# A transformer layer in one kernel: where the reciprocal square roots of its two norms are made

## The reference

```
q = [x@Wq1, x@Wq2]   (2 x 16 heads of 16)     k, v = x@Wk, x@Wv
p = softmax(causal(q @ k^T / 4))              y = y1 - sigmoid(x@Wlam) * y2,  y1, y2 = halves of p @ v
x1 = norm(x + y @ Wo)
shared = (silu(x1@G) * (x1@U)) @ Down   (1024 wide)
routed = the same at 128 wide, times the sum of the softmaxed two largest router logits
out = norm(x1 + shared + routed)
norm(z) = (z - mean(z)) / sqrt(var(z) + 1e-5)   over the 256 features of a token
```

## Time and profile before

| | |
|---|---|
| time, median of 3 runs | 504.79 us |
| profiled execution, its time | 504.88 us |
| its span, first to last instruction | 503.1 us |
| TensorE busy | 424.3 us (84%) |
| VectorE busy | 329.1 us (65%) |
| ScalarE busy | 239.1 us (48%) |
| GpSimd busy | 226.7 us (45%) |
| one iteration, 2 to 6 | 54.2 us |
| mean granted TensorE clock | 0.95 |

### The profile page before, as it was taken

How to read it: one execution, slowest core, us unless ns; L and a number is a source line. 1 busy time by engine, 2 the same in 40 slices (tenths; PEclk the granted TensorE clock), 3 DMA queues, 4 the chain that set the end, 5 groups by cost and what they waited for, 6 DMA issues and landing times.

```text
span 503.1 us, 10443 instructions
## 1 busy us (share of the span) xinstructions
PE 424.3 (84%) x4008; PEld 337.4 (67%) x4008; DVE 329.1 (65%) x875; ACT 239.1 (48%) x532; POOL 226.7 (45%) x283
## 2 busy tenths in 40 slices
PE   4107597799999999999899999999999988997983
PEld 4106335676688758876798668865887578766983
DVE  3504615974478577877687677857786769676674
ACT  4601284337435672548334843576255821582240
POOL 8201466427435572547434743656254721373040
PEclk9756779889999999999999999999999999999998
DMA  8892496129603680249112940377024910000000
GB/s 290 188 123 49 126 137 150 44 75 124 89 4 114 91 121 23 75 92 135 51 42 78 141 90 12 107 97 119 20 79 74 133 46 0 5 2 22 1 23 21
DMA packets 34355, 40.43 MB, mean 80 GB/s; under 512 B 3840, under 2 KB 27904, under 8 KB 34048
## 3 DMA queue, kind: packets, MB, share of 16 engines
q1 hardware_dynamic: 34304, 39.75, 43.2%
HBM read 27.94 MB, written 11.53 MB: 78 GB/s over the span
## 4 chain that ended last, share of the span: by engine, by line
PE 69%; DVE 15%; DMA 5%; ACT 5%; issue 4%; POOL 2%; SPq 1%; DVEq 0%
PE ybank L734 10%; PE ff L622 9%; PE ff L624 8%; PE ff L623 8%; DVE neg_max L990 8%; PE ring L706 5%; PE ring L685 5%; DMA k_stack<-qk_parts_dram 4%; PE ybank L622 4%; PE ybank L747 3%; PE ring L710 3%; PE ybank L623 3%; PE ybank L624 3%; ACT prob L469 2%; PE ring L680 2%
## 5 line engine op out<-in xcount | busy, mean ns | idle before, releaser
L990 DVE TENSOR_REDUCE neg_max<-ring 128x2 f32<-128x512 f32 (+3 forms) x176 | 105.7, 635 | 39.2 <-PE ring L685 37.4
L469 ACT ACTIVATE prob<-ring 128x512 f32<-128x512 f32 x192 | 100.8, 612 | 15.9 <-PE ring L706 15.8
L370 POOL TENSOR_TENSOR h_lo<-h_full,h_hi 128x256 fp32r<-128x256 f32 x72 | 53.0, 736 | 107.7 <-ACT h_hi L429 107.7
L380 POOL TENSOR_SCALAR_AFFINE_SELECT prob<-prob 128x512 f32<-128x512 f32 x128 | 83.9, 679 | 33.9 <-ACT prob L469 33.9
L622 PE MATMUL ff<-x1T_hi,wg_lo 128*128 128x256 f32 x288 | 85.8, 298 | 1.2 <-DVE h_full L1006 1.2
L624 PE MATMUL ff<-x1T_hi,wg_hi 128*128 128x256 f32 x288 | 80.5, 279 | 0.0
L623 PE MATMUL ff<-x1T_lo,wg_hi 128*128 128x256 f32 x288 | 80.5, 279 | 0.0
L680 PE MATMUL ring<-mask_b,ident_b 128*128 128x128 bf16 (+2 forms) x176 | 45.2, 257 | 32.7 <-DMA k_stack<-qk_parts_dram 26.8
L477 ACT ACTIVATE gate_t<-ff 128x256 f32<-128x256 f32 x72 | 27.6, 384 | 77.2 <-PE ff L624 74.5
L685 PE MATMUL ring<-k_stack,q_stack 96*128 96x256 bf16 (+3 forms) x512 | 60.5, 239 | 0.0
L734 PE MATMUL ybank<-prob,v_ones 128*32 128x256 f32 (+1 forms) x1024 | 56.1, 338 | 4.2 <-issue 2.8
(11 more groups left out here) (150 smaller groups left out, 947.9 us busy)
## 6 DMA issues: line engine op xcount, KB each, us to landing
q_stack<-qk_parts_dram SPq DMA_DIRECT2D x48, 256.0 KB, 9.2
qk_parts_dram<-parts SPq DMA_DIRECT2D x72, 128.0 KB
k_stack<-qk_parts_dram SPq DMA_DIRECT2D x8, 384.0 KB, 15.0
xt_raw<-xT SPq DMA_DIRECT2D x8, 256.0 KB, 2.9
k_stack<-qk_parts_dram SPq DMA_DIRECT2D x8, 256.0 KB, 11.8
xz<-x SPq DMA_DIRECT2D x8, 256.0 KB, 3.3
out<-xz SPq DMA_DIRECT2D x8, 256.0 KB, 2.2
prob<-w_gu SPq DMA_DIRECT2D x1, 1152.0 KB, 7.7
```

Of the source, the lines that this page charges most:

```text
L370: pool.tensor_tensor(h_lo[:, n, :], h_full[:, n % RING, :], h_hi[:, n, :].bitcast(F32), ALU.subtract).then_inc(h_lo_done, 1)
L380: pool.affine_select(out=v, in_=v, compare_op=ALU.is_ge, fill=0.0, base=0, pattern=[[0, 2], [HALF, 2], [0, 2], [1, HALF]], channel_multipl ...
L469: act.activation(prob[:, g % RING, u, :], ring[u][:, :], ACT.Exp, scale=SCALE).then_inc(exp_done, 1)
L990: dve.tensor_reduce(neg_max[:, columns.start:columns.stop, i], ring[u % RING][:, 0:len(columns) * keys].rearrange("p (h k) -> p h k", k=keys),
```

## The change

GpSimd makes both reciprocal square roots. A constant tile `minus_half` (128x2, filled with -0.5) is added, and the root is one TENSOR_TENSOR with the operation `pow` of variance + EPS and that tile. The seed, the Newton steps and the shift of VectorE go; VectorE keeps statistics, aggregation and the application of the second norm.

```diff
+            def first_scale(b):
+                base = b * SCALE_STEPS
+                pool.wait_ge(attn_step, (b + 1) * ATTN_STEPS)
+                if not is_first(b):
+                    pool.wait_ge(x1_done, b * TT)
+                pool.tensor_scalar(ln_t[:, 0, 0, :], ln_mv[:, 0, :, 1], 1.0, EPS, ALU.mult, ALU.add).then_inc(norm1_scale, 1)
+                pool.tensor_scalar(ln_t[:, 0, 2, :], ln_mv[:, 0, :, 0], -1.0, 0.0, ALU.mult, ALU.add).then_inc(norm1_scale, 1)
+                pool.wait_ge(norm1_scale, base + 2)
+                pool.tensor_tensor(ln_t[:, 0, 1, :], ln_t[:, 0, 0, :], minus_half[:, :], ALU.pow).then_inc(norm1_scale, 1)
+                pool.wait_ge(norm1_scale, base + 3)
+                pool.tensor_tensor(ln_shift[:, :], ln_t[:, 0, 2, :], ln_t[:, 0, 1, :], ALU.mult).then_inc(norm1_scale, 1)
+
+            def second_scale(b):
+                pool.wait_ge(norm2_step, (b + 1) * LN_STEPS)
+                if not is_first(b):
+                    pool.wait_ge(out_done, b * TT)
+                pool.tensor_scalar(ln_t[:, 1, 0, :], ln_mv[:, 1, :, 1], 1.0, EPS, ALU.mult, ALU.add).then_inc(norm2_scale, 1)
+                pool.wait_ge(norm2_scale, 2 * b + 1)
+                pool.tensor_tensor(ln_t[:, 1, 1, :], ln_t[:, 1, 0, :], minus_half[:, :], ALU.pow).then_inc(norm2_scale, 1)
...
             def iteration(i, has_next, has_prev, has_last):
+                if has_prev:
+                    first_scale(i - 1)
                 if has_next:
                     split_xt(i + 1)
...
                     causal(i, range(g, g + 1))
+                    if has_last and g == SCALE_GROUP:
+                        second_scale(i - 2)
...
-            h_rests(B - 1, range(FF_UNITS))
+            first_scale(B - 1)
+            h_rests(B - 1, range(SCALE_UNIT))
+            second_scale(B - 2)
+            h_rests(B - 1, range(SCALE_UNIT, FF_UNITS))
+            second_scale(B - 1)
...
-                act.wait_ge(attn_step, (b + 1) * ATTN_STEPS)
+                act.wait_ge(norm1_scale, (b + 1) * SCALE_STEPS)
...
-                        if u < NEWTON + 4:
-                            first_norm_step(u, *before)
+                        if u == 0:
+                            norm_mean(0, *before)
...
-                        elif g <= NEWTON:
-                            norm_newton(1, *norm2)
-                        elif g == NEWTON + 1:
-                            second_norm_end(i - 2, *norm2)
+                        elif g == SCALE_GROUP + 2:
+                            second_norm_end(i - 2)
```

More of the change, by code:

```diff
@@ L52 @@
 ROUTER_STEPS = 5
-NEWTON = 3
-LN_STEPS = 2 * TT + 3 + (TT + 1) * NEWTON
-NORM1_STEPS = LN_STEPS + 1
+LN_STEPS = 2 * TT
+NORM1_STEPS = LN_STEPS
+SCALE_STEPS = 4
+SCALE_GROUP, SCALE_UNIT = 3, 2
 V_COLS = 32
@@ L87 @@
 EPS = 1e-5
-RSQRT_SEED = float(0x5F3759DF - 0x400000)
 F32 = mybir.dt.float32
@@ L92 @@
 BF16 = mybir.dt.bfloat16
-I32 = mybir.dt.int32
 ALU = mybir.AluOpType
@@ L146, in build_layer @@
         ln_shift = sb("ln_shift", [P, TT])
-        ln_i = sb("ln_i", [P, 2, TT], I32)
+        minus_half = sb("minus_half", [P, TT])
         gate_t = sb("gate_t", [P, RING, T])
@@ L207, in build_layer @@
         attn_step = sem("attn_step")
+        norm1_scale, norm2_scale = sem("norm1_scale"), sem("norm2_scale")
         gu_full, gate_th_done, gate_done, h_done, h_hi_done, h_lo_done = (sem(n) for n in ("gu_full", "gate_th_done", "gate_done", "h_done", "h_hi_done", "h_lo_done"))
@@ L333, in _ @@
             pool.memset(v_ones[:, :, :, HEAD_DIM:V_COLS], 0.0).then_inc(const_step, 1)
-            pool.wait_ge(const_step, STACKS + 4)
+            pool.memset(minus_half[:, :], -0.5).then_inc(const_step, 1)
+            pool.wait_ge(const_step, STACKS + 5)
             for m in (ident, ident_b):
@@ L940, in norm_mean @@
                     step(dve.bn_aggr(ln_mv[:, which, t, :], ln_stats[:, which, t, :]))
[L942 to L975, removed]
             def split_xt(b):
@@ L1090, in second_norm_start, with second_norm_end @@
                 norm_mean(1, step, settle)
[L1091 to L1095, removed]
+            def second_norm_end(b):
+                dve.wait_ge(norm2_scale, 2 * (b + 1))
                 z = xz[b % X_SLOTS]
@@ L1171, in _ @@
             first = stepper(attn_step, B * ATTN_STEPS - NORM1_STEPS + TT)
-            for n in range(NEWTON + 4):
-                first_norm_step(n, *first)
+            norm_mean(0, *first)
             x1T_second(B - 1)
@@ L1185, in _ @@
                     second_norm_start(B - 2, *norm2)
[L1186 to L1189, removed]
+                if n == SCALE_UNIT + 2:
+                    second_norm_end(B - 2)
             add_shared(B - 1, ring[0])
@@ L1193, in _ @@
             second_norm_start(B - 1, *norm2)
-            for _ in range(NEWTON):
-                norm_newton(1, *norm2)
-            second_norm_end(B - 1, *norm2)
+            second_norm_end(B - 1)
 _OUT = ((B, T, D), "float32")
```

## The result

The changed kernel takes 519.73 us (median of 4 runs, 519.17 to 520.39), against 504.75 us of the kernel before (4 runs too, one more than stood ahead of the prediction). The ratio is 1.030, 95% interval [1.028, 1.033]. So it is 3% slower: the forecast had the sign, but 3.7 us of loss where 15.0 were measured. The profiled run took 520.19 us with a span of 518.4 us, 15.3 us longer than before.

The account below looks back on a forecast made before the run. PE was taken to bound the kernel in iterations 2 to 6, VectorE in iteration 1. Losses of 10.2 + 0.5 us less gains of 7.0 made net +3.7 on 504.88 us: 508.5 us, range 503.5 to 521.

Parts of the forecast that it names:

- the rival on the slow power: GpSimd's pow is a software routine costing 1.3 us or more on two columns: 514.2 to 520.5 us; chance 0.17.
- The wait that is added: GpSimd's input split queues behind the first norm's root, so PE stalls 0.74 + C in each of iterations 2 to 6.
- C: Time of GpSimd's four new instructions, from the aggregation's end to the split's start: 1.3 us, with pow at 0.5.
- that half of the rival: A one-time load of about 6 us at pow's first call, stalling iteration 1: 514.5 us; chance 0.03.
- the formula 7C - 5.4: Net change of the whole kernel in us, losses less gains, as a function of C; break-even at 0.77 us.
- Iteration 1: VectorE bound it; without the norm steps and the half clock level it gains 4.2 - C, here 2.9 us.
- Iteration 7: No next batch waits behind the root; the sixth row maximum comes sooner, a gain of 1.0 us.
- The end: Behind the last iteration, three norm places gain 0.7, 1.0 and 1.4 us.
- The second phase: The second norm's root is covered in GpSimd's queue behind group 3; its later application costs 0.1 us an iteration.
- no difference: Rival for the whole kernel: C between 0.6 and 1.0, giving 503.7 to 506.5 us; chance 0.17.
- the faster case: Rival: GpSimd's chain is cheap, C below 0.77, and VectorE's relief wins; 503.0 us at C = 0.5; chance 0.13.
- the absorbed stall: Rival: the split isn't late for PE or the iteration gives the stall back; 498.3 us; chance 0.03.

Follow-up runs that it names:

- e2: The changed kernel with 17 extra matmuls that nobody reads ahead of the first projection of iterations 1 to 6: 513.66 us.
- e3: The changed kernel with mult in place of pow in both norms, so the root is left out: 509.41 us.
- e4: The kernel before, with GpSimd only waiting for VectorE's aggregation of the first norm ahead of the input split: 510.74 us.
- e1: The changed kernel with GpSimd's input split put ahead of the first norm's root: 496.47 us, 0.984 of the kernel before.
- e7: The kernel of e1 with the second norm's root one group earlier in the second phase (SCALE_GROUP 2, not 3): 498.66 us.
- e10: The changed kernel with only the first norm's root on GpSimd, behind the input split, and the second norm as before the change: 499.61 us.
- e11: The kernel of e1 measured again, on the same chip as e12: 499.95 us, 0.989 of the kernel before.
- e12: The kernel of e7 measured again, on the same chip as e11: 499.18 us, 0.986 of the kernel before.
- e5: The changed kernel with 8 extra matmuls that nobody reads ahead of the first projection of iterations 1 to 6: 513.03 us.

## Why the prediction was right or wrong

**The step that failed** is in the rival on the slow power: "from stalls near 4 us PE may fall to the half level, as it did behind the sparse stretch of iteration 1". I took the forecast stall, 2.04 us, as too short for the clock. It was 2.08, and the level fell in each of six iterations for 3.4 us. The term is missing from the sum: 5 x 1.7 = 8.5 us in iterations 2 to 6, and 1.7 us in iteration 1. The runs show it from both sides, by work put into the gap (e2) and by a gap 0.5 us shorter (e3). The kernel before had the sign of it. Its own half level began at 97.6 us in iteration 1, behind these two waits of PE:

```profile
95.64 0.23 PE L680 MATMUL ring<-mask_b,ident_b 128*128 128x128 bf16 x1 [0.69 <-DVE neg_max L990]
...
97.46 0.23 PE L680 MATMUL ring<-mask_b,ident_b 128*128 128x128 bf16 x1 [1.43 <-DVE neg_max L990]
```

From 94.95 to 97.46 PE was busy for 0.40 us of 2.51, so it had been idle for 2.1 us, the length of the stall that I forecast and not near 4 us. I should have priced the half level behind any new stall of that size.

**The wait that is added**: right. The end of the aggregation sets the start of the split, and PE waits for it; the stall was 2.08 against 2.04, since the chain was 0.2 us longer than I took it and PE's last unit ended 0.2 us later. e4 shows the wait without the work and e1 the work without the wait.

**C**: 1.5 us, without the semaphore, against 1.3. `pow` at 0.69 was nearer to the low end, as chosen, but above the 0.5 of the sum. Its first use took 0.71 us and began 0.08 us after the instruction before it (91.41 us), so nothing like a load of 6 us stands there; that half of the rival is refuted. Of the fixed costs 0.19 us for each of the three other instructions was right. The second scalar instruction follows the first by 0.27 us, not 0.1, and a gap is 0.08 us where I took 0.14; these two errors nearly cancel. With this C the formula 7C - 5.4 gives +5.1 us; the missing clock term adds 10.2, and their sum is the 15.3 measured. That it fits to the tenth is partly luck: iterations 2 to 6 came out 0.4 us below their part of it (19.8 against 20.2) and the start 0.3 us above.

**Iteration 1**: direction right, a gain of 1.0 us instead of 2.9, for the same reason. I had said that no stretch at the half clock would be left. PE stood idle for 2.5 us and fell to the half level as before the change, for 3.4 us instead of 6.8. Where the stall is gone, the iteration gains 5.0 us (e1), 4.9 (e7, e10), 3.7 (e11) and 3.0 (e12); the last two have a half level at another place.

**Iteration 7**: 0.9 us against 1.0.

**The end**: 2.9 us against 3.1. The very end, in the changed profile:

```profile
513.82 0.25 DVE L969 BATCH_NORM_AGGREGATE ln_mv<-ln_stats 128x2 f32<-128x6 f32 x2
515.16 0.74 DVE L1090 TENSOR_SCALAR xz<-xz,ln_mv,ln_t 128x256 f32<-128x256 f32 x2 [1.09 <-POOL ln_t L376]
```

1.09 us stand between aggregation and application, where the earlier trace rows have 2.39: a gain of 1.3, with 1.4 forecast. My split of the rest was off a little: by e10 the first norm of batch 7 gives 0.2 to 0.4 us of the end, not 0.7.

**The second phase**: right. `second_scale` is hidden behind group 3, at 297.87 to 298.84, before a select that waits for ScalarE until 299.10:

```profile
298.14 0.70 POOL L376 TENSOR_TENSOR ln_t<-ln_t,minus_half 128x2 f32<-128x2 f32 x1
299.10 1.31 POOL L401 TENSOR_SCALAR_AFFINE_SELECT prob<-prob 128x512 f32<-128x512 f32 x2 [0.26 <-ACT prob L498]
```

The 0.1 us an iteration for `second_norm_end` can't be told from nothing (e7 against e12).

**The rivals**: a slow `pow` is out by its row; no difference, the faster case and the absorbed stall are out by the time. The measured 519.7 us lies inside the range to 521, but by the wrong mechanism: the range reached there for a chain of 3 us.

## What to carry to other kernels

An engine's in-order queue turns a wait into a wait of all that stands behind it: before you give an engine a new job that waits, look for the instruction queued behind it that another engine needs, and put that one first. Here the exchange of two calls turned a kernel 3% slower than its predecessor into one 1.1 to 1.6% faster. And where TensorE has been dense, work out a new gap twice: at its length alone, and with the matmuls that run at the half level behind it. Here a gap of 2.08 us cost 3.8 us, and taking it to 1.58 us in six iterations, half a microsecond of another engine's work, was worth ten microseconds in all.

## What the runs showed of the hardware

- `pow` of 128x2 on GpSimd takes 0.69 us (16 instructions, 0.688 to 0.708), a product or a scalar operation of that size 0.19.
- TensorE's granted clock fell to 0.50 behind idle times of 1.86 us (4 of 5), 2.08 (5 of 5) and 2.85 us (5 of 5) before the first projection of iterations 2 to 6, in otherwise dense work, and never there behind 1.58 us or less (e3, e5, e4: 15 iterations). It came up to 1.2 us after work had begun again, or before that, and lasted 3.4 us, once 6.8.
- At two other places the same idle time came before a fall in some profiles and not in others: 1.37 us in iteration 1 (fell in e11 and e12, held in e1, e2, e5, e7, e10), and 0.6 and 1.46 us close together at the end of iteration 7 (fell in 9 of 14).
- Matmuls without use in the gap kept the level: 17 of them (iteration 4 of e2 has 1.87 us more PE busy time than before the change) made an iteration 1.8 us shorter than in the changed kernel.
